# Mamba and top-2 experts on one core: u*D by a diagonal matmul, expert outputs scattered in the expert stage, gates and all steps at new places

## The reference

```
x = x + ln(attention(ln(x)))
x = x + ln(experts(ln(x)))
```

```
h[t] = exp(delta[t] * A) * h[t-1] + delta[t] * B[t] * u[t]
y[t] = sum over the 16 states of h[t] * C[t]
y    = (y + u * D_skip) * silu(res)
out  = y @ out_w
```

## Time and profile before

| what | value |
|---|---|
| time, median of 3 runs | 6693.94 us (6691.05 to 6695.23) |
| the profiled execution, its own time | 6735.03 us |
| its span in the profile | 6733.1 us |
| busy, share of the span | PE 80%, PEld 44%, DVE 78%, ACT 57%, POOL 66% |
| mean granted TensorE clock | 0.878 of full |
| DMA | 1297.88 MB, mean 193 GB/s |
| attention phase | to 5816 us |
| expert phase | 5816 to 6318 us |
| combine phase | 6318 us to the end |

### The profile page before, as it was taken

How to read it: one execution, slowest core, us unless ns; L and a number is a source line. 1 busy time by engine, 2 the same in 40 slices (tenths; PEclk the granted TensorE clock), 3 DMA queues, 4 the chain that set the end, 5 groups by cost and what they waited for, 6 DMA issues and landing times. The chain is left out here.

```text
span 6733.1 us, 71525 instructions
## 1 busy us (share of the span) xinstructions
PE 5418.0 (80%) x16640; PEld 2989.0 (44%) x16640; DVE 5240.0 (78%) x6883; ACT 3841.4 (57%) x6622; POOL 4435.8 (66%) x2993
## 2 busy tenths in 40 slices
PE   4788888888888888888888888898888887699400
PEld 1344444444444444444444444444444444466300
DVE  4898888988898989888888888888888984111255
ACT  3566666666666666666666666666666653111255
POOL 2677777777777777777777777777777775100375
PEclk8898999998998989888998999989998987799755
DMA  7666666666665666666666666666666563122342
GB/s 254 220 222 215 218 215 214 222 217 217 217 220 208 220 217 218 214 205 205 212 211 205 211 210 210 205 211 210 206 208 215 200 207 100 50 87 87 96 145 87
DMA packets 492099, 1297.88 MB, mean 193 GB/s; under 512 B 59310, under 2 KB 216624, under 8 KB 490560
## 3 DMA queue, kind: packets, MB, share of 16 engines
q1 hardware_dynamic: 440960, 1219.82, 53.8%
q10 hardware_dynamic: 26048, 38.95, 1.7%
q0 software_dynamic: 24576, 33.72, 1.6%
HBM read 1206.19 MB, written 119.54 MB: 197 GB/s over the span
## 5 line engine op out<-in xcount | busy, mean ns | idle before, releaser
L509 POOL TENSOR_TENSOR st<-st,C_rows 128x1024 f32<-128x1024 f32 x1024 | 2486.2, 2437 | 794.0 <-DVE st L1078 790.5
L1078 DVE TENSOR_TENSOR_SCAN st<-dA,drive 128x1024 f32<-128x1024 f32 x1024 | 2339.8, 2285 | 201.5 <-ACT dA L718 67.1
L885 PE MATMUL y<-st,ident 128*128 128x512 f32 x4096 | 2138.7, 663 | 350.6 <-POOL st L509 342.4
L718 ACT ACTIVATE dA<-delta,a_neg 128x511 f32<-128x511 f32 x2048 | 1372.1, 713 | 849.4 <-DVE st L1078 723.3
L885 PEld LDWEIGHTS y<-st,ident 128*128 128x128 f32 x4096 | 832.2, 210 | 1416.6 <-issue 922.0
L1050 DVE TENSOR_TENSOR drive<-du,B_rows 128x1024 f32<-128x1024 f32 x1024 | 1259.7, 1230 | 112.3 <-DMA B_rows<-bc_rows 28.4
L1458 POOL DMA_INDIRECT rows<-expert_out,idx_c x256 | 267.3, 1044 | 626.0 <-DVE idx_c L1505 555.2
L859 PE MATMUL pre_bank<-e_abs,in_w 128*128 128x512 f32 x1024 | 565.9, 691 | 77.5 <-DVE u L1027 74.6
L838 PE MATMUL post_bank<-d_w,gT 128*128 128x256 f32 x2048 | 453.7, 380 | 27.4 <-issue 26.6
L596 POOL DMA_INDIRECT expert_in<-tb,idx x256 | 257.1, 1004 | 311.8 <-DVE idx_all L1233 235.6
L838 PEld LDWEIGHTS post_bank<-d_w,gT 128*128 128x128 f32 x2048 | 388.0, 190 | 111.6 <-issue 60.2
(11 more groups left out here) (203 smaller groups left out, 8103.6 us busy)
## 6 DMA issues: line engine op xcount, KB each, us to landing
B_rows<-bc_rows SPq DMA_DIRECT2D x1024, 512.0 KB, 3.8
C_rows<-bc_rows SPq DMA_DIRECT2D x1024, 512.0 KB, 5.2
xin<-in_x SPq DMA_DIRECT2D x32, 512.0 KB, 7.1
expert_in<-gT ACTq DMA_DIRECT2D x8, 2048.0 KB, 27.5
xn_rows<-xin SPq DMA_DIRECT2D x32, 512.0 KB, 6.2
h<-xn_rows SPq DMA_DIRECT2D x32, 512.0 KB, 7.5
x_res<-in_x SPq DMA_DIRECT2D x32, 512.0 KB, 6.4
x_rows<-x_res SPq DMA_DIRECT2D x32, 512.0 KB, 6.5
```

The lines of the kernel that those rows point to most:

```text
L509: pool.tensor_tensor(tile[:, :, :], tile[:, :, :], bc[1][k % ROWS[1]][:, :, :], ALU.mult)\
L718: return act.activation(dA[k % 2][:, j, 1:L], delta[par][:, c, 1:L], ACT.Exp, scale=a_neg[:, c, n:n + 1])
L885: last = pe.matmul(Y[:, :], ident[:, :], st[k % RING][:, j, :], start=pair == 0 and j == 0, stop=pair == CU - 1 and j == 1)
L1078: dve.tensor_tensor_scan(st[k % RING][:, :, :].rearrange("p a l -> p (a l)"), dA[k % 2][:, :, :].rearrange("p a l -> p (a l)"), DR[:, :, : ...
```

## The change

**u*D on TensorE.** A tensor `d_diag` [128, 4, 128] is made once by ACT from the identity and D. At the start of each chunk TensorE multiplies `d_diag` of the chunk with u into Y (start=True); the 16 halves of the pairs are added to it. DVE's gate is one instruction.

```
+            for c in range(KI):
+                last = act.activation(d_diag[:, c, :], ident[:, :], ACT.Copy, scale=d_skip[:, c:c + 1])
...
                     if pair == 0:
-                        pe.wait_ge(*(scan_y.at(f"b{c - 1}", b) if c else scan_y.at(f"b{KI - 1}", b - 1)))
+                        pe.wait_ge(*(scan_y.at(c - 1, b) if c else scan_y.at(KI - 1, b - 1)))
+                        if k == 0:
+                            pe.wait_ge(*pre_act.at("u", b))
...
+                        pe.matmul(Y[:, :], d_diag[:, c, :], u[par][:, c, :], start=True, stop=False)
...
                 dve.wait_ge(*scan_sum.at(CU * (c + 1) - 1, b))
-                dve.scalar_tensor_tensor(Y[:, :], u[par][:, c, :], d_skip[:, c:c + 1], Y[:, :],
-                                         ALU.mult, ALU.add).then_inc(scan_y.did(f"a{c}"), 1)
-                dve.wait_ge(*scan_y.at(f"a{c}", b))
                 dve.tensor_tensor(u[par][:, c, :], Y[:, :], g[par][:, c, :], ALU.mult)\
```

**Zeros.** The experts' outputs now go to `rank_rows`: 2 x 16384 rows of 256, first and second choice of each token, 32 MB. SP clears 1 MB of it per sample from a tile of zeros:

```
+                zero_row = zeros[:, :].unsqueeze(1).to_broadcast([P, 2 * TT * D // zeros.shape[1], zeros.shape[1]])
+                sp.dma_start(yr_zero_v[b].rearrange("p (a r) -> p a r", r=zeros.shape[1]), zero_row)\
+                    .then_inc(rank_rows_zeroed, 16)
```

```
+                    slots_meta(n, i)
                     dve.wait_ge(*e_mm2.at(n, i))
-                    dve.wait_ge(stored[n % 2], 16 * (NB // 2) * i + 16 * (n // 2 + 1))
-                    for tile in range(0, TB, 2):
-                        last = dve.tensor_copy(O[n % 2][:, tile:tile + 2, :],
-                                               OB[tile // 2][:, :].rearrange("p (a d) -> p a d", a=2))
+                    dve.wait_ge(*e_meta.at(f"w_slot{n}", i))
+                    for tile in range(TB):
+                        last = dve.tensor_scalar(O[n % 2][:, tile, :],
+                                                 OB[tile // 2][:, (tile % 2) * D:(tile % 2 + 1) * D],
+                                                 w_slot[:, tile:tile + 1], None, ALU.mult)
...
+        def _(pool):
+            e_sent.credit(pool)
+            with pool.Fori(0, NE // 2) as i:
+                for n in range(NB):
+                    pool.wait_ge(*e_out.at(n, i))
...
+                    for tile in range(TB):
+                        pool.indirect_dma_start(
+                            out=yr_dram, in_=O[n % 2][:, tile, :], in_offset=None,
+                            out_offset=bass.IndirectOffsetOnAxis(ap=dest_i[n % 2][:, tile:tile + 1], axis=0),
+                            bounds_check=2 * NTOK - 1, oob_is_err=False).then_inc(stored, 16)
+                    pool.wait_ge(stored, 16 * TB * NB * i + 16 * TB * (n + 1))
+                    pool.sem_inc(e_sent.did(n), 1)
```

```
+                for half in range(TT // 2):
+                    for c in range(2):
+                        last = pe.matmul(total[n % H][:, 2 * half:2 * half + 2, :].rearrange("p t d -> p (t d)"), ident[:, :],
+                                         rows[n][:, c, 2 * half:2 * half + 2, :].rearrange("p t d -> p (t d)"),
+                                         start=c == 0, stop=c == 1)
...
+            turns(dve, ((2, add), (0, stats)))
...
+            turns(act, ((0, normalise), (2, store)))
```

More of the change, by code:

```diff
@@ L200, in attention_phase @@
         h = sb("h", [P, TT, D])
-        tb = sb("tb", [P, TT, D])
+        tb_wide = sb("tb", [P, TT, DW])
+        tb = tb_wide[:, :, 0:D]
+        wts = tb_wide[:, :, D:D + 2]
+        top_f = tb_wide[:, :, D + 2:D + 4]
+        token = tb_wide[:, :, D + 4]
+        next_token = sb("next_token", [P, TT])
+        zeros = sb("zeros", [P, 2 * D])
         s = tb
@@ L1055, in gate, with gates @@
                 dve.wait_ge(*scan_sum.at(CU * (c + 1) - 1, b))
-                dve.scalar_tensor_tensor(Y[:, :], u[par][:, c, :], d_skip[:, c:c + 1], Y[:, :],
-                                         ALU.mult, ALU.add).then_inc(scan_y.did(f"a{c}"), 1)
-                dve.wait_ge(*scan_y.at(f"a{c}", b))
                 dve.tensor_tensor(u[par][:, c, :], Y[:, :], g[par][:, c, :], ALU.mult)\
-                    .then_inc(scan_y.did(f"b{c}"), 1)
+                    .then_inc(scan_y.did(c), 1)
+            def gates(b, par):
+                at = iter((30, 56, 77))
+                for c in range(KI - 1):
+                    yield next(at)
+                    if isinstance(b, int) and b == 0 and c == 0:
+                        dve.wait_ge(post_weights_in, 16 * len(POST_IN))
+                    gate(b, par, c)
             def scan(b, par, *stages):
@@ L1081, in recur @@
                                            ALU.mult, ALU.add).then_inc(scan_h.did(k), 1)
-                run_slots(stages, (chunk_done, recur, ahead))
+                run_slots((gates(b, par), *stages), (nothing, recur, ahead))
                 if isinstance(b, int) and b == 0:
@@ L1248, in expert_phase @@
         w2 = [sb(f"w2_{i}", [P, KE, D]) for i in range(2)]
-        X = [sb(f"X{i}", [P, TB, D]) for i in range(2)]
+        X = [sb(f"X{i}", [P, TB, DW]) for i in range(2)]
+        expert = sb("expert", [P, 1])
+        mine = sb("mine", [P, TB, 2])
+        w_mine = sb("w_mine", [P, TB, 2])
+        w_slot = sb("w_slot", [P, TB])
+        dest = sb("dest", [P, TB])
+        dest_i = [sb(f"dest_i{i}", [P, TB], U32) for i in range(2)]
         XT = [sb(f"XT{i}", [P, KD, BLK]) for i in range(2)]
@@ L1334, in _ @@
                 steps.credit(act)
-            for half in range(2):
-                act.sem_inc(stored[half], 16)
             with act.Fori(0, NE // 2) as i:
@@ L1446, in _, with add @@
-            turns(sp, ((3, store), (0, load)))
-            for n in range(G):
-                sp.wait_ge(out_stored[n], 16 * (S // G + 1))
+                sp.dma_start(rows[n][:, :, :, :], yr_v[G * i + n]).then_inc(rows_loaded[n], 16)
+            turns(sp, ((0, load),))
+        @block.tensor
+        def _(pe):
+            c_sum.credit(pe)
+            def add(n, i):
+                pe.wait_ge(rows_loaded[n], 16 * (i + 1))
+                pe.wait_ge(*(c_out.at(n - H, i) if n >= H else c_out.at(n - H + G, i - 1)))
+                for half in range(TT // 2):
[3 more added lines that the diff above has]
+                                         start=c == 0, stop=c == 1)
+                last.then_inc(c_sum.did(n), 1)
+            turns(pe, ((0, add),))
@@ new lines, in _, with stats, add @@
+        @block.vector
+        def _(dve):
+            for steps in (c_stats, c_out):
+                steps.credit(dve)
+            dve.wait_ge(x1_loaded, 16 * S)
+            def stats(n, i):
+                dve.wait_ge(*c_sum.at(n, i))
+                for tile in range(TT):
+                    last = dve.bn_stats(stat[n][:, tile, :], total[n % H][:, tile, :])
+                last.then_inc(c_stats.did(f"stats{n}"), 1)
+                dve.wait_ge(*c_stats.at(f"stats{n}", i))
+                dve.sem_inc(carried_dve_c, 1)
+                for tile in range(TT):
+                    last = dve.bn_aggr(mv[n][:, tile, :], stat[n][:, tile, :])
+                last.then_inc(c_stats.did(f"aggr{n}"), 1)
+            def add(n, i):
+                dve.wait_ge(*c_normed.at(n, i))
+                x1 = x1_all[:, bass.ds(G * i + n, 1), :, :].rearrange("p s t d -> p (s t d)")
+                dve.tensor_tensor(x1, total[n % H][:, :, :].rearrange("p t d -> p (t d)"), x1, ALU.add)\
+                    .then_inc(c_out.did(n), 1)
+            turns(dve, ((2, add), (0, stats)))
@@ L1450, in _ @@
         @block.gpsimd
         def _(pool):
[L1452 to L1461 removed]
+            c_shift.credit(pool)
@@ L1463, in _ @@
+            turns(pool, ((0, scale_and_shift),))
         @block.scalar
         def _(act):
-            for steps in (c_scaled, c_r, c_normed):
-                steps.credit(act)
-            def scaled(n, i):
-                act.wait_ge(gathered[n], 16 * 2 * TT * (i + 1))
-                act.wait_ge(*ready.at(n, i))
-                for tile in range(TT):
-                    last = act.activation(rows[n][0][:, tile, :], rows[n][0][:, tile, :], ACT.Copy,
-                                          scale=w_c[n][:, tile, 0:1])
-                last.then_inc(c_scaled.did(n), 1)
@@ L1477, in power @@
[L1477 to L1487 removed]
+            c_normed.credit(act)
```

295 lines of the change are left out of this document (153 added, 142 removed).

## The result

The changed kernel takes **6354.87 us** (median of 4 runs, 6353.4 to 6362.86) where the kernel before took 6692.72 beside it: ratio 0.9497, 95% interval 0.9481 to 0.9514. The forecast was 6306, its range 6180 to 6480. The profiled execution took 6355.55 us, its span is 6353.8.

A forecast was written before the change was run, and what follows sets the result against it. In attention no engine was full, DVE nearest the bound and waiting at the gate; gather issue bound the combine. Attention -163, setup +3, combine -228 make -388: 6735.0 to 6347, or 6306 from the median 6693.9; range 6180 to 6480.

The forecast's parts named there:

- the experts: Expert stage: added waits for scatters and metadata cost nothing, covered by a block of TensorE; blocks still 14.7 us.
- the gate's wait: Attention: DVE's 5.8 us per sample of waiting before the gate shrinks by 4.3 through earlier slot numbers and moved places.
- So DMA binds at 4.4, or TensorE at 6.9: Combine, per sample: transfers limit at 4.4 us, or TensorE at 6.9 if its clock stays low; 5.2 taken.
- the chain of 7.5 us for two samples: Combine: statistics, POOL's and ACT's small steps, then the add take 7.5 us with hops, 3.8 per sample.
- the 41 us: Whole kernel: profiled execution lies 41 us over the runs' median; the same difference was subtracted from the forecast.
- I take these two as exposed, +1.7: Attention: two of four diagonal matmuls for u*D fall where TensorE is full, adding 1.7 us per sample; ends 0 and 6.9.
- rival B: Attention: TensorE becomes the bound and takes back what DVE gives; attention as before, 6469 us; chance 0.20.
- the ring of four: Attention: four st buffers make the recurrence wait for the sum four pairs back, the next stall after the gate's wait.
- Zero fill: +0.5: Attention: SP's 1 MB of zeros per sample delays the B_rows load, adding 0.5 us per sample; ends 0 and 3.1.
- C: Attention: the long wait goes with all that hangs on it, half clock too; -9 per sample, 6181 us; chance 0.13.
- D: Combine: TensorE stays at 1.2 GHz since it waits for a load before each burst; 6359 us; chance 0.13.
- E: Attention: second FFN product's new place at slot 10 delays a sum, diagonals at half clock; +11.0 per sample, 6821 us; chance 0.04.

The follow-up runs named there:

- before_again: The kernel before, unchanged, run again with a new profile: 6740.0 us, ratio 0.9997.
- after_again: The changed kernel, unchanged, run again beside the kernel before on a chip where that takes 6738.6: 6359.8 us, ratio 0.9445.
- both_old: The changed kernel with u*D back on DVE and all old places of steps and gates: 6461.2 us, ratio 0.9596.
- places_old: The changed kernel with all fifteen lists of places and the gates' slots put back to old, u*D still on TensorE: 6446.6 us, ratio 0.957.
- scatters_spread: places_old with the last six of POOL's eight scatters moved from slot 43 to 45 through 51, SP's wait for them from 47 to 58: 6318.0 us.
- scatters_later: scatters_spread with the eight scatters at slots 45, 45, 46, 46, 48, 48, 49, 51: 6306.8 us, ratio 0.9418.
- combine_one: The changed kernel with TensorE adding only the first choice's rows in the combine, two matmuls per sample for four: 6364.9 us, ratio 0.9518.
- late_new: The changed kernel with old places for everything but the late stage, which keeps its new ones; u*D on TensorE: 6691.7 us, ratio 0.9939.

## Why the prediction was right or wrong

The side and the range held; the forecast was 49 us too low. The miss lies ahead of the combine, once like is set against like. Of the mechanisms, that of the experts held, and that of the gate's wait in the main; u*D and the limit of the combine came out otherwise than written.

**Combine: right for another reason than written.** The forecast had 193 us from the last eviction on (421 - 228) and 31 steps of 5.2; it is 148 and 3.70. The step that failed is "So DMA binds at 4.4, or TensorE at 6.9": neither does. The prediction's own third term binds, the chain of 7.5 us for two samples, 3.8 each; it measures 7.46. The 4.4 came from 354 GB/s, scaled from one stretch of attention that was not its fastest (336 GB/s; 2680 to 2690 us moved 354); the stage moves 418. The Trainium skill ("Perfetto Trace Analysis", "Roofline") bounds a core that runs alone by its 16 DMA engines, some 435 GB/s together; the 418 lie 4% under that, and an estimate of 1.57 MB at that figure, 3.6 us, stays below the chain's 3.8. The clock was 0.50 for the first 10 us only, so the third of the way up to 6.9 wasn't needed, and TensorE's 3.6 (97.87 of 100 us at 3.70 a sample) hides under the chain. The first chain (29.0 us from the last eviction to the first add, against 5.5 + 4.4 + 6 + 12 = 27.9) was sized well. That gives 45 us more than forecast against the profile; but the 41 us by which the profiled execution lies over the median were taken over as a constant. They are time of the old combine on one kind of chip. Where the kernel before takes 6693 to 6699 its combine is 377.7 us, so the stage saves 377.7 - 146.9 = 231 there (from an execution 13 us over its median). The forecast's 228 fits by luck: a new stage 45 us too long, taken from an old one 43 us too long.

**Attention: -163 forecast, -104 to -109 measured** (31 periods, before to after and before_again to after_again; both_old to after_again is 101 in total).
- u*D: 3.0 off DVE was right in size (3.1), and 3.4 on TensorE too (3.4 busy). The step that failed is "I take these two as exposed, +1.7": 2.6 to 2.8 of the 3.1 came back, so -1.3 x 32 = -42 should have been -15. This is rival B, for this one term. The trace of before had two signs of it: both engines at 88%, and the gate's wait, which ends on TensorE. The Trainium skill's rule ("Perfetto Trace Analysis", "Identifying the Most-Contended Engine"), by which weight loads at 48% would leave TensorE room and the term at 0, errs in the same direction and further: in places_old PEld is at 49% of the window and DVE's waits for TensorE grew by 3.0 us per sample with the diagonals.
- The gate's wait: -4.3 was right in size for what hung on the scatters, but not in its parts. scatters_spread shortens the period by 4.0, and scatters_later by 4.1, without the 2.3 us of earlier slot numbers and the 3.5 us of DVE work ahead of the gate that the prediction added up to nearly 7.3. What it left out of the sum is the half clock, 5.4 us in the sample above. The kernel after kept only 2.7 (87 us) of the 4.0. Probably the other new places took it, for they brought waits with them: 41.1 us for r_late and 39.5 + 16.7 for tb, 3.6 per sample together, none of them in the list of before; no run removes these waits alone. The prediction named the ring of four as what is late next (93.7 against 15.0, 2.9 per sample, seen), and left the new order of the late stage at nothing.
- Zero fill: +0.5, measured 0 (the period of both_old is 0.2 below that of before_again). B_rows waits stayed small, 5.5 us in the window.
- Setup: +3, measured 7.6 to 8.5. DVE's first work with the loaded a_neg starts at 41.8 us where it was 35.3, and D_skip is now among the loads that this waits for; that it is this load was not tried.

**Experts: right.** Blocks are (6205.73 - 5738.59)/31 = 15.1 us apart, before (6312.44 - 5840.70)/31 = 15.2. The eviction waits for TensorE's product as before, not for the scatters:

```profile
5738.59 1.66 DVE L1469 TENSOR_SCALAR O<-bank,w_slot 128x256 f32<-128x256 f32 x4 [6.93 <-PE bank L1381]
...
6205.73 1.66 DVE L1469 TENSOR_SCALAR O<-bank,w_slot 128x256 f32<-128x256 f32 x4 [6.51 <-PE bank L1381]
```

**The rivals.** B holds for u*D and not for the stage. C didn't come: the ring took the place of the long wait, as the forecast had it. D is refuted, the granted clock is 0.99. The Trainium skill's rule ("TensorE: Matmul & The Clock Gate", "HAM oscillation — how this bites in real kernels") would have the clock drop before every burst that waits for a load. In the kernel after there are hardly any gaps, so it isn't put to the test. combine_one, with TensorE waiting 37.6 of 100 us for the sums' release and 62% busy, shows 0.91, at the high level most of the time; waits for a load before each burst no run here has. E's place may be what late_new shows (h waits 90.5 us), but in the change as made the out_w product moved ahead of it.

## What to carry to other kernels

A block of DMA issues at one slot stalls what stands behind it on its engine: ask first what it costs to spread that block, alone; here two lists gave 107 us in the old kernel, as much as fifteen lists and a new matmul. Ask too at which clock TensorE runs behind such a stall: in the sample shown that was the larger part of the wait. Work moved from one engine at 88% to another at 88% can come back nearly whole: here 3.1 us were spared and 0.3 to 0.5 kept, some 0.9 once the long wait was mostly gone. When no engine's time and no transfer changes the pace, add up the chain that goes round through several engines. And before a profile is scaled to a median, find the stage in which they differ, and whether the change removes that stage.

## What the hardware showed that I had not expected

- Loads of 1 MB and stores of 0.5 MB together move 417 to 418 GB/s at a DMA share of 1.03, where the stretch of the earlier trace rows had 336 at 0.95. The share can read over 1; scaling GB/s by it gave a limit 15% below what was moved.
- The same gather stage of 256 indirect DMAs differs by 42 to 48 us between chips (420.1 and 425.3 against 377.7), while the new combine doesn't: 146.7 to 147.0 us in all runs but combine_one.
- Behind a wait of 2.06 us for POOL TensorE ran at half clock, and the same group of four records took 3.78 us instead of 1.98. The whole wait at the gate was 7.24 us there and 0.62 without that.
- Through 100 us with TensorE 62% busy the granted clock was 0.91.
